# Gated recurrence and feed-forward in eight chunks: chunk 3's turned x gets its own place, steps around chunks 0 to 4 and the last chunks change their order

## What is computed

```python
pre = layernorm(x) @ W + b                       # 256 -> 1024
i, f, o, z = split(pre, 4)
i = 10 * tanh((i + input_bias) / 10); f = -softplus(f); o = sigmoid(o); z = tanh(z)
for each step t:                                 # along the sequence
    m_next = max(f + m, i)
    i_s = exp(i - m_next); f_s = exp(f + m - m_next)
    c = f_s * c + i_s * z;  n = f_s * n + i_s
    h = o * c / (n + 1e-6);  m = m_next
x = x + h / rms(h) * scale
g = layernorm(x) * gamma + beta
x = x + 0.5 * (silu(g @ w1 + b1) @ w2 + b2)      # 256 -> 1024 -> 256
```

## Time and profile before

| | |
|---|---|
| median of 3 runs | 306.15 us (306.0 to 306.26) |
| the profiled execution | 304.67 us, of which 302.9 us span from the first to the last instruction |
| TensorE busy | 293.1 us, 97% of the span, 1728 matmuls |
| VectorE busy | 256.4 us, 85% |
| ScalarE busy | 235.7 us, 78% |
| GpSimd busy | 131.4 us, 43% |
| mean granted TensorE clock | 0.994 |

### The profile page before, as it was taken

The page is one execution under the profiler, slowest core; times in us unless marked ns, Lnnn a source line. Parts: engine busy times, 40 slices in busy tenths (PEclk is TensorE's granted clock), DMA queues, the critical chain, the costliest instruction groups (busy, mean ns, idle before and its releaser), DMA issues.

```text
span 302.9 us, 4764 instructions
## 1 busy us (share of the span) xinstructions
PE 293.1 (97%) x1728; PEld 254.8 (84%) x1728; DVE 256.4 (85%) x470; ACT 235.7 (78%) x382; POOL 131.4 (43%) x133
## 2 busy tenths in 40 slices
PE   7899999999999899999999999999999989999996
PEld 5688788877898689968899889988799888889896
DVE  3999887999999799999997899698999899683521
ACT  2688988799989974999693994979884978866910
POOL 3052045001098419911993129601698777135000
PEclk9999999799999999999999999999999999999999
DMA  7990003000000422043004400240000552302201
GB/s 261 344 335 0 0 0 72 0 0 2 0 1 2 70 70 72 0 92 118 0 3 69 139 2 0 36 106 0 0 3 2 102 106 55 51 35 55 52 35 69
DMA packets 15206, 17.87 MB, mean 59 GB/s; under 512 B 832, under 2 KB 14416, under 8 KB 15056
## 3 DMA queue, kind: packets, MB, share of 16 engines
q1 hardware_dynamic: 10368, 12.07, 11.6%
q0 software_dynamic: 4400, 4.73, 9.6%
q10 hardware_dynamic: 416, 0.79, 0.7%
HBM read 8.67 MB, written 4.19 MB: 42 GB/s over the span
## 4 chain that ended last, share of the span: by engine, by line
DVE 35%; POOL 23%; PE 22%; issue 15%; DMA 3%; ACT 0%; POOLq 0%; DVEq 0%; SPq 0%
POOL rows L1195 6%; POOL g L1180 4%; DVE y_lo L898 4%; DVE g L866 3%; PE mm_ps L260 3%; PE mm_ps L258 3%; PE mm_ps L259 3%; DVE rows L874 3%; DVE bn L879 3%; POOL r L1188 3%; DVE rec L822 2%; DVE rec L807 2%; DMA rows<-x 2%; POOL rrms L1166 2%; PE z_ps L355 2%
## 5 line engine op out<-in xcount | busy, mean ns | idle before, releaser
L355 PE MATMUL z_ps<-w_hi,y_hi 128*128 128x256 f32 x200 | 57.3, 286 | 0.9 <-DVE rows L912 0.6
L357 PE MATMUL z_ps<-w_hi,y_lo 128*128 128x256 f32 x200 | 56.3, 282 | 0.0
L356 PE MATMUL z_ps<-w_lo,y_hi 128*128 128x256 f32 x200 | 56.3, 282 | 0.0
L614 ACT ACTIVATE y<-mm_ps,b_all,unit 128x512 f32<-128x512 f32 x58 | 44.6, 768 | 3.8 <-PE mm_ps L349 3.1
L898 DVE TENSOR_TENSOR y_lo<-y,y_hi 128x512 fp32r<-128x512 f32 x56 | 38.5, 707 | 6.2 <-ACT y_hi L617 6.2
L342 PE MATMUL mm_ps<-gt_hi,w_hi 128*128 128x512 f32 x124 | 39.8, 402 | 0.3 <-ACT y L606 0.3
L355 PEld LDWEIGHTS z_ps<-w_hi,y_hi 128*128 128x128 f32 x200 | 37.7, 188 | 1.7 <-DVE rows L912 0.8
L349 PE MATMUL mm_ps<-gt_lo,w_hi 128*128 128x512 f32 x124 | 38.9, 395 | 0.0
L258 PE MATMUL mm_ps<-xt_hi,wg_hi 128*128 128x512 f32 x96 | 38.4, 400 | 0.0
L356 PEld LDWEIGHTS z_ps<-w_lo,y_hi 128*128 128x128 f32 x200 | 37.7, 189 | 0.3
L259 PE MATMUL mm_ps<-xt_lo,wg_hi 128*128 128x512 f32 x96 | 37.9, 395 | 0.0
(11 more groups left out here) (203 smaller groups left out, 732.2 us busy)
## 6 DMA issues: line engine op xcount, KB each, us to landing
rows<-b_bc POOLq DMA_DIRECT2D x8, 512.0 KB, 5.1
out<-rows SPq DMA_DIRECT2D x15, 256.0 KB, 2.1
rows<-x SPq DMA_DIRECT2D x7, 512.0 KB, 6.6
q<-fc_q SPq DMA_DIRECT2D x2, 1024.0 KB, 11.3
wg_raw<-fc_scales SPq DMA_DIRECT2D x1, 1024.0 KB, 8.5
wg_raw<-w_gates SPq DMA_DIRECT2D x1, 512.0 KB, 5.8
wg_raw<-w_gates ACTq DMA_DIRECT2D x1, 512.0 KB, 6.1
w_lo<-q POOLq DMA_DIRECT2D x1, 512.0 KB, 4.6
```

The lines of the kernel that those rows point to most:

```text
L355: pe.matmul(dst, hi, w2_hi[:, k], start=(k == 0), stop=False)
L356: pe.matmul(dst, hi, w2_lo[:, k], start=False, stop=False)
L357: return pe.matmul(dst, lo, w2_hi[:, k], start=False, stop=(k == KF - 1))
L614: act.activation(y[:, j % YBUFS], fc1_bank(c, j), ACT.Silu, bias=b1_all[:, j:j + 1], scale=unit[:, j:j + 1]).then_inc(silu_done, 1)
```

## The change

Chunk 3's turned x is kept in `y_more` (a tile so far used only for the low parts of y of chunk 6) and not in `xt_hi`, `xt_lo`, which chunk 2's gates still read. So x_turned(3) and x_high(3) can stand in the midst of chunk 2's gates. The first two gate tiles of chunk 3 go ahead of g_turned(0); shifted_bias comes behind it, in another bank of `z_ps`, and its last three columns between fc1's first tiles. h of chunk 2 is turned behind all eight fc1 tiles of chunk 1 (before: six), h of chunk 3 behind five tiles of chunk 2 (before: two). One gate tile of chunk 3 goes ahead of h_turned(1). The product i times z of chunk 2 goes from VectorE to GpSimd. VectorE's and ScalarE's lists follow; in the lists of chunks 5 to 7, `final(4, 1)` goes ahead of `residual(6)`, g of chunk 6 is turned one block of fc2 later, and a few y_low change places.

```diff
         def xt(c):
-            return [y_hi[:, 0:KD], y_lo[:, 0:KD]] if c == 1 else [xt_hi[:], xt_lo[:]]
+            if c == 1:
+                return [y_hi[:, 0:KD], y_lo[:, 0:KD]]
+            return [y_more[:, 0:KD], y_more[:, KD:2 * KD]] if c == 3 else [xt_hi[:], xt_lo[:]]
...
-                    if c == 0 and j in (4, 5):
+                    if c == 0 and j == 4:
+                        pe.wait_ge(w1_scaled, KD)
+                    elif c == 0 and j == 5:
                         pe.wait_ge(b1_ready, 2)
...
-            gates(2, range(2, GJ))
+            gates(2, range(2, 5))
             x_turned(3)
-            shifted_bias()
+            gates(2, range(5, GJ))
+            gates(3, range(0, 2))
             g_turned(0)
-            gates(3, range(0, 2))
-            fc1(0, range(KF))
+            shifted_bias(range(0, 5))
+            for j in range(3):
+                fc1(0, [j])
+                shifted_bias([5 + j])
+            fc1(0, range(3, KF))
+            gates(3, range(2, 3))
             h_turned(1)
-            gates(3, range(2, GJ))
+            gates(3, range(3, GJ))
             fc2_first()
             fc2(0, [1])
+            fc2(0, [3], range(0, KF // 2))
             g_turned(1)
-            fc2(0, [3])
+            fc2(0, [3], range(KF // 2, KF))
             fc1(1, range(0, 2))
             x_turned(4)
-            fc1(1, range(2, 6))
+            fc1(1, range(2, KF))
             h_turned(2)
-            fc1(1, range(6, KF))
...
                 x_turned(t + 1)
-                fc1(t - 2, range(0, 2))
+                sooner = range(0, 5 if t == 4 else 2)
+                fc1(t - 2, sooner)
                 h_turned(t - 1)
-                fc1(t - 2, range(2, KF))
+                fc1(t - 2, range(len(sooner), KF))
...
-            fc2(5, [1], range(0, KF // 2))
+            fc2(5, [1], range(0, 5))
             g_turned(6)
-            fc2(5, [1], range(KF // 2, KF))
+            fc2(5, [1], range(5, KF))
```

ScalarE's list (scalar block) follows TensorE's:

```diff
             square_sums(0)
-            gates(2, range(2, 3))
             act.wait_ge(w1_scaled, 1)
             act.activation(w1_hi[:, 1], w1_f, ACT.Copy).then_inc(w1_rounded, 1)
-            for n in range(TT):
-                gates(2, range(n + 3, n + 4))
-                x_normalised(3, range(n, n + 1))
-            gates(2, range(7, GJ))
+            x_normalised(3)
+            gates(2, range(2, 5))
             x_high(3)
+            gates(2, range(5, GJ))
             g_normalised(0)
+            gates(3, I_TILES)
             g_high(0)
...
-                gates(3, I_TILES[u:u + 1])
...
             x_high(4)
-            silu(1, range(2, 6))
+            silu(1, range(2, KF))
             square_sums(2)
-            silu(1, range(6, KF))
...
-                silu(t - 2, range(0, 2))
+                sooner = range(0, 5 if t == 4 else 2)
+                silu(t - 2, sooner)
                 square_sums(t - 1)
-                silu(t - 2, range(2, KF))
+                silu(t - 2, range(len(sooner), KF))
```

On GpSimd one step is new, ahead of `rms_root(1)`:

```diff
             ln2_root(0)
+            input_times_z(2)
             rms_root(1)
```

More of the change, by code:

```diff
@@ L433, in h_turned, with shifted_bias @@
                     ins.then_inc(ht_ready, 1)
-            def shifted_bias():
+            def shifted_bias(tiles):
                 pe.wait_ge(w1_scaled, KD)
-                pe.wait_ge(gate_done, at(1, 8, 6))
-                for j in range(KF):
+                for j in tiles:
                     for k in range(KD):
                         f = slice(j * P, (j + 1) * P)
-                        ins = pe.matmul(z_ps[:, 0, 0, j:j + 1], w1_f[:, f] if k else w1_hi[:, 0, f].bitcast(F32),
+                        ins = pe.matmul(z_ps[:, 1, 0, j:j + 1], w1_f[:, f] if k else w1_hi[:, 0, f].bitcast(F32),
                                         col[:, COL_BETA + k:COL_BETA + k + 1], start=(k == 0), stop=(k == KD - 1))
-                ins.then_inc(beta_w1, 1)
+                if tiles[-1] == KF - 1:
+                    ins.then_inc(beta_w1, 1)
             def idle_passes(count):
@@ L575, in x_high @@
                     act.wait_ge(pre_done, at(0, 8, 8))
-                elif c >= 3:
+                elif c == 4:
+                    act.wait_ge(pre_done, at(2, 8, 8))
+                elif c >= 5:
                     act.wait_ge(pre_done, at(c - 1, 8, 8))
@@ L987, in _ @@
             maximum(1, range(KD))
+            g_low(0)
+            denominators(1, range(KD))
+            divisor(1)
             dve.wait_ge(beta_w1, 1)
-            dve.tensor_tensor(b1_all[:], z_ps[:, 0, 0, 0:KF], unit[:], ALU.mult).then_inc(b1_ready, 1)
+            dve.tensor_tensor(b1_all[:], z_ps[:, 1, 0, 0:KF], unit[:], ALU.mult).then_inc(b1_ready, 1)
             dve.wait_ge(b1_ready, 1)
             dve.tensor_tensor(b1_all[:], b1_all[:], col[:, COL_B1:COL_B1 + KF], ALU.add).then_inc(b1_ready, 1)
-            denominators(1, range(0, 1))
-            g_low(0)
-            denominators(1, range(1, KD))
-            divisor(1)
             numerators(1)
@@ L1001, in _ @@
             y_low(0, range(0, 4))
-            input_times_z(2)
             dve.wait_ge(w2_rounded, 2)
@@ L1008, in _ @@
             h_scaled(1)
-            y_low(0, range(4, 6))
+            y_low(0, range(4, KF))
             residual(1)
-            y_low(0, range(6, 7))
             ln2_sums(1)
-            y_low(0, range(7, KF))
             ln2(1)
@@ L1028, in _ @@
             x_low(4)
-            y_low(1, range(2, 4))
+            y_low(1, range(2, 6))
+            final(0, 0)
+            final(0, 1)
+            y_low(1, range(6, KF))
             mean_square(2)
-            final(0, 0)
             h_scaled(2)
-            y_low(1, range(4, 5))
             residual(2)
-            y_low(1, range(5, 6))
-            final(0, 1)
             ln2_sums(2)
-            y_low(1, range(6, 7))
             ln2(2)
-            y_low(1, range(7, KF))
             maximum(3, range(KD))
@@ L1058, in _ @@
                     final(t - 3, 0)
+                    final(t - 3, 1)
+                    y_low(t - 2, range(2, 4))
                 else:
@@ L1078, in _ @@
                 mean_square(t - 1)
-                if t == 4:
-                    final(t - 3, 1)
-                y_low(t - 2, range(2, 3))
+                if t > 4:
+                    y_low(t - 2, range(2, 3))
                 h_scaled(t - 1)
-                y_low(t - 2, range(3, 4))
+                if t > 4:
+                    y_low(t - 2, range(3, 4))
                 residual(t - 1)
@@ L1102, in _ @@
             mean_square(6)
-            y_low(5, range(0, 1))
+            y_low(5, range(0, 2))
             h_scaled(6)
             final(4, 0)
-            y_low(5, range(1, 3))
+            y_low(5, range(2, 3))
+            final(4, 1)
             residual(6)
-            final(4, 1)
             y_low(5, range(3, 4))
@@ L1125, in _ @@
             residual(7)
-            y_low(6, range(2, 4))
+            y_low(6, range(2, 5))
             ln2_sums(7)
-            y_low(6, range(4, 5))
             ln2(7)
```

## The result

The changed kernel took 308.22 us (median of 10 runs, 306.87 to 309.58), the kernel before 305.46 us beside it (10 runs, 304.42 to 306.26): a ratio of 1.0103, 95% interval 1.0082 to 1.0125. It is 1.0% slower where 0.8% faster was forecast. The profiled execution took 309.52 us with a span of 307.7, against 304.67 and 302.9. The executions of the kernel before lie at two levels, 304.3 to 305.4 us with a mean granted clock of 0.993 or more and 305.8 to 306.5 us with 0.988 or 0.989; the 306.15 of the prediction was the upper, and later medians of before are 304.6 to 304.7.

A forecast was written before the change was run, and what follows sets the result against it. VectorE was taken to set the pace from 58 to 104 us, TensorE from 140 to 242 us. Gains of 1.75 + 0.8 = 2.55 us gave 302.1 us profiled, 303.6 us against the median; range 302.2 to 305.7 us.

The forecast's parts named there:

- the last ends at about 60.3: TensorE, chunk 0: the last bias matmuls among fc1's first three tiles end at about 60.3 us.
- the wait of about 1.0 us for b1: VectorE, done with divisor(1) at 59.4 us, waits about 1.0 us for b1 ahead of numerators(1).
- the +0.4 of the sum: VectorE's lead from 72 us on: 1.14 us of product saved less 0.75 us lost, 0.4 us.
- Rival 2: From 50 to 58 us, the early edit gives back the slow clock: 1.7 us more gained, 301.9 us; chance 0.04.
- The hold by GpSimd's product: Chunk 2's product on GpSimd holds b1's second step until 62.0 us, so numerators(1) starts 0.8 us later than before.
- rival 1: GpSimd does not hold VectorE up, or less: lead 1.5 us at 72 us, end at 302.5 us; chance 0.10.
- h_turned(1): TensorE waits nearly 2 us for chunk 1's h, then wins it back; nothing at the end.
- h_turned(2) and chunk 4's gates: TensorE's 1.18 us wait goes, leading 2.0 us; chunk 4's gates then wait for ScalarE, leaving 1.0 us.
- h_turned(3): TensorE's 0.90 us wait for `xt_lo` at chunk 3's h goes: plus 0.9 us, lead 1.9 us.
- Chunk 3's mean square: VectorE waits 1.4 and 1.0 us there; 0.65 us taken as its lateness at g_low(3), costing TensorE 0.2 us.
- rival 3: Late square sums' 2.4 us idle reach x_turned(6) in full, tail brings only 0.3 us: 304.8 us; chance 0.18.
- The last chunks: fc2_both(5): waits of 0.77 us for a final and 0.40 us for y_low go, about 0.5 remains: plus 0.8 us.

The follow-up runs named there:

- run 4: Changed kernel with 128 columns instead of one in each bias matmul (b1 has other values): 306.04 us, ratio 1.0028 to the kernel before.
- run 5: Changed kernel with all 16 bias matmuls in one piece behind g_turned(0), ahead of chunk 0's fc1 tiles: 306.34 us, ratio 1.0055 to the kernel before.
- run 8: Changed kernel with 128-column bias matmuls and VectorE's w2_f held until GpSimd has made nr: 304.8 us, ratio 0.9999 to the kernel before.
- run 6: Changed kernel with VectorE's w2_f held until GpSimd has made nr of chunk 0: 305.25 us, ratio 1.0013 to the kernel before.
- run 2: Kernel before with only the later h_turned(2) and h_turned(3) and VectorE's and ScalarE's orders around chunks 2 and 3's mean squares: 305.55 us, ratio 1.0031.
- run 1: Kernel before with only the part of the change up to x_turned(4): 308.46 us, ratio 1.0104.
- run 10: Changed kernel, bias matmuls in one piece, w2_f behind nr, chunk 2's product back on VectorE, chunk 3's h behind two tiles: 303.01 us, ratio 0.9928 to before.
- run 11: As run 10, but h of chunk 3 turned behind three tiles of fc1(2): 302.3 us, ratio 0.9894 to the kernel before.
- run 3: Kernel before with only the last chunks' edits (final(4, 1) sooner, g of chunk 6 later, y_low moves): 304.0 us, ratio 0.9973.

## Why the prediction was wrong

- **The step that failed: "the last ends at about 60.3" and the wait of about 1.0 us for b1.** It took an fc1 tile among the bias columns at 1.17 us. At the half clock it took 2.28 us, and each pair of bias matmuls 0.7 instead of 0.44 (59.35 to 60.06). The columns were done 5.7 us late and VectorE idled 5.43 us. numerators(1) came 5.25 us later than before instead of 0.8; with the 1.14 us of the product, the +0.4 of the sum was -4.1. These are figures of the profiled execution; a median one is 1.3 us shorter. Rival 2 had the same columns in sight but only as a gain: I read the half clock as something that the change would break up, while it kept one-column matmuls and put work of the bound engine behind them. Runs 4, 5 and 8 show it, and so does the table behind run 8.
- **The 1.4 us of the late g of chunk 0 were no term at all.** Removing VectorE's 1.52 us wait at 49.98 let w2_f start 0.07 us ahead of nr. The wait that I booked as pure gain was the cover of a small GpSimd instruction. I had the hold for the big product and did not look for others. VectorE's end of divisor(1), 59.4 in the prediction, was 60.7 by it. Run 6 prices it, with what it does to the clock, at 2.7 us.
- **The hold by GpSimd's product was right** in place and kind (runs 4, 5 and 8; 2.0 us where no wait covers it), and rival 1 wrong. The Trainium skill ("SBUF — State Buffer", SBUF: two separate sides) calls the pair's port an exclusive lock; the trace agrees both ways, 2.17 us for a VectorE row of 128x8 and 2.26 us for a GpSimd row of 128x4. b1's first step, which reads `z_ps`, kept its 0.16 us.
- **h_turned(1)** was right in kind: 1.47 us in run 4 by its bracket, nearly 2 forecast; in the changed kernel TensorE was itself late, and 0.26 is left.
- **h_turned(2) and chunk 4's gates** held: no wait, then 0.87 by starts for ScalarE (0.9 to 1.0 forecast). In run 8 the gates began at 102.49, a lead of 1.39 for 2.0.
- **h_turned(3): plus 0.9, as said.**
- **Chunk 3's mean square: minus 0.2 was minus 1.0 to 1.6.** The idle time was there (0.59 + 1.17 and 0.44 more behind it, forecast 1.4 + 1.0), but "some of that is time in which it was held up by GpSimd anyway, so I take 0.65" had nothing behind it. This is rival 3, and its full figure was the better reading.
- **Chunk 6's gates, 0.63 us, were not foreseen.** VectorE's finals wait 1.15 us at 172.62 for a transfer that GpSimd starts there, so y_low and a silu come late. Run 2, the middle alone, has no such wait; run 1, the early part alone, and runs 10 and 11, with chunk 3's old order, have none either. So it takes chunk 3's new order together with another part; which one was not tried.
- **The last chunks:** 0.8 us by run 3's ratio, as forecast, but by other items: the final's 0.77 went, the 0.40 stayed whole, and 0.3 came later on. By waits that is 0.5; its profiled execution is 0.7 us shorter.
- The sum went wrong by size and not by one step alone: with the early premises repaired (run 8) the kernel stands level with before, 304.8 beside 304.58 us, and not 2.55 below it. The middle ate the rest: TensorE's lead at x_turned(6) was 0.35 us (162.69 against 163.04), forecast 1.75, and chunk 6's gates took it.
- The base was off too: 306.15 us was the upper level of the kernel before. Against the lower level the same sum gives 302.1 us, which makes the miss larger.

## What to carry to other kernels

Before a wait is booked as a gain, look at what ran beside the idle engine: here a small GpSimd instruction lived on it, and 0.34 us of wait put back were worth 2.7 us. If the clock fell behind some piece of work before, expect that it may again where that piece is moved (here it did), and put nothing there that the bounding engine waits for. When a wait is to be filled by moving a step, move it by the length of the wait: one tile for 0.9 us won 1.0 us by the ratios (run 11), three tiles, together with VectorE's new order, lost 0.3% (run 2).
